# Small vector operations of an attention and expert kernel moved from VectorE to GpSimd, with the orders of all engines redrawn

## The reference

```python
x = x + xattn0(layernorm(x), ctx)   # 16 heads of 8, relative-position bias, mask, softmax
x = x + ffn0(layernorm(x))          # low rank 128 -> 32 -> 512, gelu, 512 -> 32 -> 128
x = x + xattn1(layernorm(x), ctx)   # 16 heads of 8, softmax without bias or mask
x = x + moe(layernorm(x))           # 16 experts, the best 8 per token, and a shared expert

def layernorm(x):  m, v = mean(x), var(x);  return (x - m) / sqrt(v + 1e-5)
def moe(x):
    s = sigmoid(l2norm(x) @ l2norm(gate).T);  w, i = top_k(s, 8);  combine = w / sum(w)
    y = (silu(x @ w_gate[e]) * (x @ w_up[e])) @ w_down[e]      # for all 16 experts e
    return sum(combine[e] * y[e]) + shared expert
```

## Time and profile before

| | us |
|---|---|
| median of 3 runs (lowest, highest) | 200.42 (199.63, 200.68) |
| the profiled execution | 201.42 |
| its span, from first to last instruction | 199.6 |
| PE busy | 169.8 (85%) |
| DVE busy | 148.3 (74%) |
| ACT busy | 133.3 (67%) |
| POOL busy | 91.1 (46%) |
| TensorE's granted clock, mean over the span | 0.964 |

### The profile page before, as it was taken

The page is one execution under the profiler, slowest core; times in us unless marked ns, Lnnn a source line. Parts: engine busy times, 40 slices in busy tenths (PEclk is TensorE's granted clock), DMA queues, the critical chain, the costliest instruction groups (busy, mean ns, idle before and its releaser), DMA issues.

```text
span 199.6 us, 4779 instructions
## 1 busy us (share of the span) xinstructions
PE 169.8 (85%) x1609; PEld 120.5 (60%) x1609; DVE 148.3 (74%) x651; ACT 133.3 (67%) x289; POOL 91.1 (46%) x110
## 2 busy tenths in 40 slices
PE   0548269998979699989789679989999999999994
PEld 0325145667658366655656356857766767869783
DVE  5390369898588967998686979898986944989461
ACT  3265046999999879998988978572687674344120
POOL 8159999989789968964230533001010020110000
PEclk9999958999999979999999979999999999999999
DMA  5255796012323862000303302300010001000000
GB/s 134 80 116 130 176 252 140 1 39 72 92 56 97 218 211 68 13 0 4 82 6 78 82 8 62 96 8 0 2 32 2 0 5 30 0 2 0 29 1 26
DMA packets 21880, 12.22 MB, mean 61 GB/s; under 512 B 3120, under 2 KB 21232, under 8 KB 21856
## 3 DMA queue, kind: packets, MB, share of 16 engines
q1 hardware_dynamic: 19776, 10.68, 21.3%
q10 hardware_dynamic: 2080, 1.24, 2.4%
HBM read 4.98 MB, written 0.54 MB: 28 GB/s over the span
## 4 chain that ended last, share of the span: by engine, by line
PE 67%; ACT 12%; DVE 10%; issue 4%; POOL 4%; DMA 2%; SPq 1%; DVEq 0%; ACTq 0%
PE bank L460 17%; PE bank L489 10%; PE bank L403 8%; PE bank L359 6%; PE bank L374 4%; PE bank L343 3%; PE bank L439 3%; PE bank L429 3%; ACT pt L1401 3%; DVE es L887 3%; ACT xn L1349 2%; PE bank L413 2%; PE bank L476 2%; PE bank L420 2%; PE bank L349 2%
## 5 line engine op out<-in xcount | busy, mean ns | idle before, releaser
L887 DVE CUSTOM_DVE_ANT_0 es<-bank,biasq 128x128 f32<-128x128 f32 x128 | 28.1, 284 | 7.8 <-PE bank L359 7.6
L1735 POOL TENSOR_TENSOR es<-es,mx 128x512 f32<-128x512 f32 x32 | 32.7, 1044 | 0.7 <-DVE mx L887 0.6
L1713 POOL TENSOR_TENSOR rstd<-ve,half 128x2 f32<-128x2 f32 x16 | 11.2, 700 | 44.3 <-DVE ve L872 43.9
L1455 ACT ACTIVATE gth<-bank 128x256 f32<-128x256 f32 (+1 forms) x36 | 13.2, 382 | 21.8 <-PE bank L460 17.1
L403 PE MATMUL bank<-pt,va 128*32 128x128 f32 x512 | 26.1, 288 | 1.5 <-ACT pt L1401 0.8
L374 PE MATMUL bank<-ident,es 128*128 128x128 f32 x128 | 19.6, 294 | 4.7 <-ACT es L1395 4.1
L460 PE MATMUL bank<-xT,wg 128*128 128x256 f32 (+1 forms) x72 | 22.9, 399 | 0.1
L893 DVE TENSOR_REDUCE mx<-bank 128x4 f32<-128x512 f32 x32 | 20.5, 679 | 2.8 <-PE bank L359 2.7
L1395 ACT ACTIVATE es<-es 128x512 f32<-128x512 f32 x32 | 19.1, 630 | 5.1 <-POOL es L1735 5.1
L460 PE MATMUL bank<-xT,wu 128*128 128x256 f32 (+1 forms) x72 | 21.4, 379 | 0.0
L489 PE MATMUL bank<-wd,hT 128*128 128x128 f32 x128 | 21.2, 291 | 0.2 <-DVE hT L1010 0.2
(11 more groups left out here) (141 smaller groups left out, 343.1 us busy)
## 6 DMA issues: line engine op xcount, KB each, us to landing
k0st<-k0p SPq DMA_DIRECT2D x24, 64.0 KB, 2.1
k1st<-k1p SPq DMA_DIRECT2D x24, 64.0 KB, 2.1
q1st<-q1p SPq DMA_DIRECT2D x24, 64.0 KB, 2.0
q0st<-q0p SPq DMA_DIRECT2D x21, 64.0 KB, 2.1
biasq<-rel_bias_scratch SPq DMA_DIRECT2D x4, 256.0 KB, 4.5
wg<-in_wg SPq DMA_DIRECT2D x1, 544.0 KB, 6.0
wu<-in_wu SPq DMA_DIRECT2D x1, 544.0 KB, 6.3
x<-in_x SPq DMA_DIRECT2D x4, 128.0 KB, 4.5
```

Source lines behind the costliest of these rows:

```text
L887: ins = dve.tensor_tensor_reduce(es[:, b, h], src[:, s * SEQ:(s + 1) * SEQ], biasq[:, h], 1.0, 3.0e38, ALU.add, ALU.min, mx[:, 0, p, b, h: ...
L1455: act.activation(gth[0:rows, n % GATES], src[0:rows, 0:TOK], ACT.Silu).then_inc(nth("gth", n), 1)
L1735: pool.tensor_tensor(es[:, b, h], es[:, b, h], mx[:, 0, p, b, h].unsqueeze(2).broadcast_to([128, 4, SEQ]), ALU.subtract).then_inc(nth(f"le ...
```

## The change

Three things move from DVE to POOL. In a norm, POOL adds the epsilon and makes the shift itself, one instruction for each batch. The split of the row maxima (`split_max`) becomes a POOL function of four instructions, and the split of the combine weights (`router_parts`) another. The maxima are no longer negated; in place of that the stacks `k1st` are cleared to -1. What is computed is otherwise unchanged. All six lists (PE, DVE, ACT, POOL, SP, and the DMAs of ACT) are written in a new order, and banks are handed out anew.

```diff
 # VectorE
                     dve.bn_aggr(mv[:, n, p, b], stats[:, n, p, b]).then_inc(nth(f"mv{n}", 2 * p + b), 1)
-                new(dve, f"mv{n}", 2 * p + 2) and dve.wait_ge(sem(f"mv{n}"), 2 * p + 2)
-                dve.tensor_scalar(ve[:, n, p], mv[:, n, p, :, 1], LN_EPS, None, ALU.add).then_inc(nth(f"ve{n}", p), 1)
-
-            def shift(n, p):
-
-                new(dve, f"rstd{n}", p + 1) and dve.wait_ge(sem(f"rstd{n}"), p + 1)
-                dve.scalar_tensor_tensor(nmr[:, n, p], mv[:, n, p, :, 0], -1.0, rstd[:, n, p], ALU.mult, ALU.mult).then_inc(nth(f"shift{n}", p), 1)
...
-            def split_max(p, b):
...
-                dve.tensor_scalar(to[:, 0], src, -1.0, None, ALU.mult).then_inc(nth(f"nm_a{b}", p), 1)
...
-                dve.tensor_copy(csp[:, :, 0], comb[:, p]).then_inc(nth("csp", 3 * p), 1)
...
 # GpSimd
             def power(n, p):
+
                 new(pool, "half", 1) and pool.wait_ge(sem("half"), 1)
+                new(pool, f"mv{n}", 2 * p + 2) and pool.wait_ge(sem(f"mv{n}"), 2 * p + 2)
+                pool.tensor_scalar(ve[:, n, p], mv[:, n, p, :, 1], LN_EPS, 1.0, ALU.add, ALU.mult).then_inc(nth(f"ve{n}", p), 1)
                 new(pool, f"ve{n}", p + 1) and pool.wait_ge(sem(f"ve{n}"), p + 1)
                 pool.tensor_tensor(rstd[:, n, p], ve[:, n, p], half[:, 0:2], ALU.pow).then_inc(nth(f"rstd{n}", p), 1)
+                new(pool, f"rstd{n}", p + 1) and pool.wait_ge(sem(f"rstd{n}"), p + 1)
+                for b in range(2):
+                    pool.tensor_scalar(nmr[:, n, p, b:b + 1], mv[:, n, p, b, 0:1], rstd[:, n, p, b:b + 1], -1.0,
+                                       ALU.mult, ALU.mult).then_inc(nth(f"shift{n}", 2 * p + b), 1)
...
+            def split_max(p, b):
...
+                pool.tensor_copy(to[:, 0], src).then_inc(nth(f"nm_a{b}", p), 1)
+                new(pool, f"nm_a{b}", p + 1) and pool.wait_ge(sem(f"nm_a{b}"), p + 1)
+                pool.tensor_tensor(rest, src, to[:, 0], ALU.subtract).then_inc(nth(f"nm_b{b}", p), 1)
+                new(pool, f"nm_b{b}", p + 1) and pool.wait_ge(sem(f"nm_b{b}"), p + 1)
+                pool.tensor_copy(to[:, 1], rest).then_inc(nth(f"nm_c{b}", p), 1)
+                new(pool, f"nm_c{b}", p + 1) and pool.wait_ge(sem(f"nm_c{b}"), p + 1)
+                pool.tensor_tensor(to[:, 2], rest, to[:, 1], ALU.subtract).then_inc(nth(f"nm{b}", p), 1)
+
+            def router_parts(p):
...
+                pool.tensor_copy(csp[:, :, 0], comb[:, p]).then_inc(nth("csp", 3 * p), 1)
...
             def clear(j, i):
-                pool.memset(stacks[j][i][:], 1.0 if j == "k1" else 0.0).then_inc(nth(f"{j}_clear", i), 1)
+                pool.memset(stacks[j][i][:], -1.0 if j == "k1" else 0.0).then_inc(nth(f"{j}_clear", i), 1)
...
-            normalize(0, 1)
-            middle("k1", 0)
```

More of the change, by code:

```diff
@@ new lines, in _ @@
+            gate_up(1, 2, 6)
+            gate_up(1, 3, 5)
+            gate_up(1, 4, 3)
+            max_turned(3, 1, 4)
+            gate_up(1, 5, 7)
+            attention_out(1, 2, 2)
+            combine_turned(1, 4)
+            gate_up(1, 6, 1)
+            gate_up(1, 7, 0)
+            spread(1, 0, 6)
+            spread(1, 1, 5)
+            spread(1, 2, 2)
+            spread(1, 3, 4)
+            gate_up(1, 8, 3)
+            down(1, 0, 7)
+            spread(1, 4, 6)
+            scores1_turned(3, 0, 0, 5, 2)
@@ new lines, in _ @@
+            spread(2, 2, 0)
+            gate_up(2, 4, 2)
+            spread(2, 3, 6)
+            spread(2, 4, 4)
+            gate_up(2, 5, 5)
+            down(2, 0, 3)
+            spread(2, 5, 7)
+            gate_up(2, 6, 1)
+            down(2, 1)
+            tokens_turned(3, 3, 2)
+            gate_up(2, 7, 0)
+            down(2, 2)
+            logits(3, 6)
+            spread(2, 6, 5)
+            down(2, 3)
+            spread(2, 7, 4)
+            gate_up(2, 8, 1)
+            down(2, 4)
@@ L846, in _ @@
-            spread(3, 7, 4)
-            gate_up(3, 4, 2)
+            gate_up(3, 1, 7)
+            down(2, 6)
+            combine_turned(3, 0)
+            gate_up(3, 2, 6)
+            down(2, 7)
+            spread(3, 0, 5)
+            spread(3, 1, 4)
+            spread(3, 2, 1)
+            down(2, 8)
+            spread(3, 3, 2)
+            spread(3, 4, 7)
+            gate_up(3, 3, 0)
+            down(3, 0, 6)
+            spread(3, 5, 5)
+            spread(3, 6, 4)
+            spread(3, 7, 3)
@@ L1092, in _ @@
             mask_values()
-            shift(0, 0)
             rel_rows()
@@ L1344, in normalize @@
             def normalize(n, p):
-                new(act, f"shift{n}", p + 1) and act.wait_ge(sem(f"shift{n}"), p + 1)
+                new(act, f"shift{n}", 2 * p + 2) and act.wait_ge(sem(f"shift{n}"), 2 * p + 2)
                 if p:
@@ L1537, in _ @@
+            copy_weights(1, 1, 0)
+            copy_values(2, 0)
+            weights0(1, 1, 2)
+            copy_weights(1, 1, 1)
+            weights0(1, 1, 3)
+            evict("k0", 2)
+            copy_weights(1, 1, 2)
+            normalize(0, 3)
+            copy_values(2, 1)
+            middle("k0", 2)
+            copy_weights(1, 1, 3)
+            middle("q0", 2)
+            normalize(1, 0)
             copy_front(3)
-            copy_values(2, 0)
-            normalize(1, 0)
+            copy_turned(1, 0)
@@ L1783, in _ @@
             less_least(0, 1, 2)
-            power(0, 2)
             less_least(0, 1, 3)
             residual(0, 0)
+            power(0, 2)
+            residual(0, 1)
             less_least(1, 0, 0)
```

969 lines of the change are left out of this document (449 added, 520 removed).

## The result

The changed kernel takes 198.0 us (median of 4 runs, 197.80 to 198.29) beside 200.22 for the kernel before: a ratio of 0.9892, with an interval of 0.9861 to 0.9922. It is 1.1% faster, where I had forecast 2.2%. The profiled execution has a span of 196.2 us, 3.4 less than before. Executions of one kernel can fall into a faster and a slower group; every ratio here compares those of the faster group alone, while a median is that of all.

What follows compares the result with a forecast made beforehand. Bound early by POOL and its chain, in the middle by DVE and ACT chains PE waits for, late by PE. +2.0 - 5.0 - 1.5 = -4.5 us gives a 195.9 us median, chance 0.50; range 192 to 202.

Steps and rivals of the forecast that it cites:

- The sign: Whole kernel: faster by over 0.5%, chance 0.63; the same 0.18, slower 0.19.
- -5.0 us: Middle, 85 to 124 us: two thirds of 7.6 us from PE's idle time and clock, bounds 0 and -7.6.
- The clock that I counted on: Middle, 85 to 124 us: PE's granted clock, 0.96 on average, could give 1.6 us.
- the 687 ns: DVE's longest epsilon beside a median of 170: a hint that DVE instructions may lengthen beside a busier POOL.
- The price x: Time of one small moved instruction on POOL, estimated at 0.30 us; 96 of them take POOL to some 120 us.
- Rival B: POOL becomes the bound of attention 0, up to 85 us; from x = 0.55 us, 203.1 us at x = 0.70; chance 0.19.
- Together -1.8 us at this point: Start: pair 1's xn 0.8 us earlier and POOL's first subtraction 1.06 us earlier.
- +2.0 us at 85 us: POOL's full stretch, 24 to 85 us: 18x - 3.4 with x = 0.30, the start's gain included.
- -3.0: 24 to 85 us: half of POOL's 6.04 us idle time absorbs the added work.
- -1.5 us from closer down products: Late stage, from 124 us: eight of 36 down products follow closely, 0.19 us each; bounds 0 and -6.8.
- A: PE is the bound whatever DVE does: middle gives 2.0 us, late stage nothing, 200.4 us; chance 0.18.
- C: After attention 0 a new wait at the head of POOL's list costs 3.0 us of the middle: 198.9 us; chance 0.13.

Runs made afterwards that it cites:

- order_only: The changed kernel's new lists with the moved small work back on VectorE; against the kernel before 1.0794, 217.22 us.
- splits_back_no_clear: The changed kernel with the eight maxima splits back on VectorE and GpSimd's clear of the fourth q1 stack moved earlier; 1.0108 to the kernel before, 203.85 us.
- old_rest: The moved work with the changed kernel's orders up to about 90 us and the old orders behind; 1.0253 to the kernel before, 205.03 us.
- after_fill: The changed kernel with the two feed-forward weight products and the second pair's value rows exchanged on PE; 0.9779 to the kernel before, 196.11 us.
- after_start: The changed kernel with the first weights turned before the value rows and three loads issued later; 0.9866 to the kernel before, 198.37 us.

## Why the prediction was right, and where it was off

**The sign: right; the middle: right in kind, too large.** I expected idle time of PE from 85 to 124 us under 3 us with the clock near 1; it is 3.49, at 1.00. The -5.0 us were too much for idle time in this stage, which gave 2.5. The clock that I counted on, 1.6, gave nothing to the sum, since PE's busy time in all is unchanged: what the fast clock saves in the middle, the slow start took.

**Why the middle gained: half right.** I put it to VectorE's relief. The move alone made things worse (PE waits 2.5 us for splits at GpSimd in the old lists). What the orders alone are worth no run shows cleanly, since `order_only` has a wait of my making. But either half taken out of the changed kernel loses more than the whole gain: the splits' move 4.2 us of span (`splits_back_no_clear`), the orders behind 85 us 7.0 (`old_rest`). The gain is that of the two together: in the new order PE waits for no split, and VectorE's maxima follow each other without them. A smaller part is that VectorE's small steps can be held by a GpSimd instruction beside them. I had named that only as a risk (the 687 ns). In the kernel before, the 80 moved steps take 17.7 us and by their medians would take 13.8, an estimate from the trace of L872, L877, L905 to L911 and L975 to L981, so some 3.9 us of them were such stretches. What the moves of the epsilon, the shift and the combine weights' split are worth by themselves no run shows.

**The price x: right in kind, too high.** 0.30 us forecast, 0.23 measured. POOL came to 111.5 instead of 120. DVE came to 132.9 instead of 131, so the work that stayed there grew by 2.3 us (148.3 - 17.7 = 130.6); the products of the context (`ct`, L899) take 442 ns each instead of 374. The Trainium skill (GPSIMD Engine Reference, 4.1 Engine selection) puts elementwise work with two inputs at about twice the time on GpSimd. Here a small step of this kind is 217 ns on GpSimd (L1697) against 175 on VectorE (L907), a ratio of 1.24: at this size the factor of two isn't there. Rival B fell on it, x being far from the 0.55 at which it begins.

**The start and GpSimd's stretch: the step that failed.** "Together -1.8 us at this point" was right for GpSimd (2.2, or 1.6 to 1.8 in the later runs) and wrong for the kernel. ScalarE's queue issued nine loads up to 24.0 us, so that its first exponential came at 24.04, and PE's bank waited for a copy of value rows behind that. I had followed GpSimd and no queue but its own. Then "+2.0 us at 85 us" took no account of TensorE: the last of the 32 subtractions ended at 90.0 us, 5.6 later than before. PE ran at 1.2 GHz to 39.7 us, against 32 before, and the scores of pair 1 came late. I never priced the two feed-forward products that the new PE list puts into the slow stretch. `after_fill` gives this its size: 2.3 of the 5.6 us, and 2.3 us of span. The other 3.3 no run takes apart. The term "-3.0", that GpSimd's idle time would take up work, went the wrong way: from 24 to 85 us GpSimd's idle time rose from 6.04 to 61.00 - 52.47 = 8.53 us. So in this stretch GpSimd waited for others more than before, and the chain through TensorE set the pace.

**Luck in the number.** 198.0 lies in the range partly because errors cancel. From the 32nd subtraction to the end the new kernel takes 196.2 - 90.0 = 106.2 us and the old one 199.6 - 84.4 = 115.2. That is 9.0 less, where my terms for the middle and the late stage add up to 6.5, and it covers most of the 3.6 us by which the first stretch was worse than my +2.0. That `after_fill` reaches 196.1 us, near my 195.9, is no support for the sum, whose parts came out otherwise.

**The late stage.** -1.5 us from closer down products did not come: they take 289 ns each after and 291 before. After 124 us PE's idle time fell by 0.75 us.

**Rivals.** A had said that the bound is PE. In its strong form (0 gain) it fell, but it had the late stage right. C's 198.9 us is nearer to the 198.0 than my forecast, but its mechanism is not what was seen: GpSimd's splits waited 1.2 us for VectorE from 85 to 124 us, behind the clear it stood another 1.85 us for a variance in any case, and PE waited for no `nm` there.

## What to carry to other kernels

Small work that is moved between engines pays, or costs, by its place in the lists: here the move alone lost 1.1%, together with the orders it gained 1.1%. Before pricing a start, follow every queue that issues into it, and ask at which clock PE will run what is drawn into it. Here work taken away in the slow stretch cost 6 us, and work exchanged for other work gained 2. Where VectorE and GpSimd both run short steps, look at whether the long ones among VectorE's end together with a GpSimd instruction.

## What the runs showed of the hardware

- Small SBUF instructions of VectorE can be held to the end of a GpSimd instruction that runs beside them: in one split 0.17 us became 0.65 beside additions and 2.38 beside an addition and a memset of 1.80 us, and moving the memset took that one back to 0.65. The Trainium skill (GPSIMD Engine Reference, 8. Key points) says that GpSimd shares its SBUF interfaces with VectorE and contends with those VectorE instructions that run in a two-port mode or have two SBUF inputs. The trace agrees in that the held steps stood beside GpSimd instructions; one of them (L900) has two inputs, and whether the two with one input (L898, L902) ran in a two-port mode no run here shows.
- Dependent steps on GpSimd start 0.28 us apart (92.90, 93.18, 93.46, 93.74 in the changed kernel) at 0.20 to 0.22 us of length, so a split takes 1.06 us there. A power of 128x2 takes 701 ns, and one of 16x1 still 606.
- In the changed kernel PE was busy from 28 to 40 us and stayed at the 1.2 GHz level to about 39.7, with the two feed-forward products in this stretch. With them exchanged for value rows the 2.4 GHz level came by 33.3 us. What of the exchange does it these runs don't separate: the products have 32 rows and the value rows 128, and PE's small gaps (0.35 and 0.56 us) moved too.
- The granted clock isn't always in the record. In `after_start` it reads 1.00 from 28 to 40 us, and the same products take 2.07 us as at 0.50. Lengths of like matmuls are the safer sign here.
